# A fused cross-attention and spline feed-forward kernel: mask work moved in front of weight sums in batch 0, banks of value and stage products exchanged, late turning in the first quad, and the seventh product ahead of the next batch's first projections

## The reference, cut to what matters

```python
kv_c = kv @ W_kvc                                  # [512, 256] per batch
q_c = q @ W_dq                                     # [512, 384]; q is the normalised x
q_nope = (q_c @ W_uq).reshape(b, lq, H, HD)        # 16 heads of 128
q_rope = _rope((q_c @ W_qr).reshape(b, lq, H, R))  # R = 64
k_nope, v = kv_c @ W_uk, kv_c @ W_uv
k_rope = _rope(kv_c @ W_kr)
scores = (q_nope @ k_nope^T + q_rope @ k_rope^T) * scale
good = (k_ids <= qs) & (k_ids >= qs - LOOKBACK)    # qs: the token's segment number
attn = softmax(where(good, scores, NEG))
out = (attn @ v).reshape(b, lq, H * HD) @ W_o      # [512, 2048] @ [2048, 1024]
```

## Time and profile before

| | |
|---|---|
| runs | 3152.68, 3148.94, 3150.11 us; median 3150.11 |
| profiled execution | 3152.13 us, span of the core 3150.3 us |
| mean granted TensorE clock | 0.968 |
| busy share | PE 94%, DVE 69%, ACT 52%, POOL 30% |
| chain that ended last | 67% of it on PE, 9% DVE, 4% ACT, 1% POOL, 1% DMA |

### The profile page before, as it was taken

One profiled execution on the slowest core, in us unless ns is written; L12 is line 12 of the kernel. 1 busy time (PEld: TensorE's weight loads), 2 busy tenths in 40 slices (PEclk: granted clock), 3 DMA queues, 4 the chain that ended last, 5 costly groups with the idle time before them and its releaser, 6 DMA issues.

```text
span 3150.3 us, 41227 instructions
## 1 busy us (share of the span) xinstructions
PE 2960.7 (94%) x13886; PEld 2390.0 (76%) x13886; DVE 2181.1 (69%) x4546; ACT 1645.4 (52%) x3220; POOL 942.7 (30%) x685
## 2 busy tenths in 40 slices
PE   8899987999999999999999999999999999999985
PEld 6777766788778877788787887788777887878762
DVE  4555655777677775777667776677757777577776
ACT  3665634555365553655445553555526554465553
POOL 6355453221412114212332114112142212321127
PEclk9999998999999999999999999999999999999995
DMA  7565655555565546455664556655465555645432
GB/s 254 184 206 184 210 204 197 186 181 175 219 230 186 174 158 257 170 182 184 219 231 171 179 176 234 210 184 179 161 250 186 184 184 210 223 163 184 148 100 13
DMA packets 178303, 592.73 MB, mean 188 GB/s; under 512 B 38304, under 2 KB 52256, under 8 KB 141744
## 3 DMA queue, kind: packets, MB, share of 16 engines
q1 hardware_dynamic: 173024, 589.21, 53.8%
q0 software_dynamic: 5072, 0.88, 0.7%
HBM read 471.31 MB, written 85.14 MB: 177 GB/s over the span
## 4 chain that ended last, share of the span: by engine, by line
PE 67%; DVE 9%; ACT 4%; issue 2%; POOL 1%; DMA 1%; ACTq 0%; SPq 0%; POOLq 0%; DVEq 0%
PE psD L2577 8%; PE psA L2498 7%; PE psC L2594 7%; PE psB L2507 5%; PE psE L2594 5%; PE psT L2564 4%; PE psA L2450 3%; PE psS L2536 3%; PE psS L2537 3%; PE psS L2549 3%; PE psS L2545 3%; PE psS L2546 3%; PE psD L2520 2%; DVE probsT_lo L1897 2%; PE psB L2450 2%
## 5 line engine op out<-in xcount | busy, mean ns | idle before, releaser
L1459 ACT ACTIVATE exps_ring<-exps_ring,neg_max 128x512 f32<-128x512 f32 x512 | 370.9, 724 | 398.7 <-DVE neg_max L1885 397.6
L1885 DVE CUSTOM_DVE_ANT_0 exps_ring<-psS,mask 128x512 f32<-128x512 f32 x512 | 352.6, 689 | 173.3 <-PE psS L2549 155.1
L1473 ACT ACTIVATE probsT_hi<-psT 128x512 fp32r<-128x512 f32 x432 | 258.1, 597 | 410.6 <-PE psT L2564 406.8
L1897 DVE TENSOR_TENSOR probsT_lo<-psT,probsT_hi 128x512 fp32r<-128x512 f32 x432 | 297.5, 689 | 174.9 <-ACT probsT_hi L1473 173.4
L1465 ACT ACTIVATE exps_ring<-exps_ring,row_sum_inverse 128x512 f32<-128x512 f32 x512 | 368.6, 720 | 48.0 <-DVE row_sum_inverse L1891 47.9
L2594 PE MATMUL psC<-w_o_product,attn_product 128*128 128x512 f32 x1260 | 344.7, 409 | 24.5 <-POOL w_o_product L1095 23.8
L2594 PEld LDWEIGHTS psC<-w_o_product,attn_product 128*128 128x128 f32 x1260 | 228.3, 192 | 72.7 <-POOL w_o_product L1095 25.3
L2594 PE MATMUL psE<-w_o_product,attn_product 128*128 128x512 f32 x1008 | 272.4, 405 | 0.0
L2564 PE MATMUL psT<-ident,exps_ring 128*128 128x128 f32 x1728 | 261.7, 274 | 10.6 <-DVE probsT_lo L1897 9.7
L2564 PEld LDWEIGHTS psT<-ident,exps_ring 128*128 128x128 f32 x1728 | 210.1, 140 | 79.7 <-issue 33.6
L2498 PE MATMUL psA<-q_c_hi,w_uq_ring 128*128 128x512 f32 x768 | 262.7, 396 | 0.1
(11 more groups left out here) (488 smaller groups left out, 6612.1 us busy)
## 6 DMA issues: line engine op xcount, KB each, us to landing
w_o_product<-w_o_split SPq DMA_DIRECT2D x190, 1024.0 KB, 5.4
w_uq_ring<-w_uq_split SPq DMA_DIRECT2D x112, 384.0 KB, 4.7
w_o_split<-w_o_product SPq DMA_DIRECT2D x28, 1024.0 KB, 5.5
w_uk_ring<-w_uk_split SPq DMA_DIRECT2D x112, 256.0 KB, 2.9
w_uv_quad<-w_uv_split SPq DMA_DIRECT2D x28, 1024.0 KB, 6.9
w_qr_sorted<-w_qr_split SPq DMA_DIRECT2D x28, 768.0 KB, 4.3
x_stage<-in_x_dram SPq DMA_DIRECT2D x32, 512.0 KB, 5.2
x_stage<-in_ctx_dram SPq DMA_DIRECT2D x32, 512.0 KB, 6.0
```

The lines of the kernel that those rows point to most:

```text
L1459: act.activation(E[:, qt, :], E[:, qt, :], ACT.Exp, scale=-1.0, bias=mx[:, i % 2, qt:qt + 1], accum_out=rs[:, i % 2, qt:qt + 1]).then_inc( ...
L1885: dve.tensor_tensor_reduce(E[:, qt, :], psS[qt % 2][:, :], mask[:, qt, :], -SCALE, BIG, ALU.add, ALU.min, mx[:, i % 2, qt:qt + 1]).then_in ...
L1897: dve.tensor_tensor(PT[1][:, :, qt * P:(qt + 1) * P], turn_bank(q, i, qt)[:, :].rearrange("p (c n) -> p c n", c=TT), hi.bitcast(F32), ALU. ...
```

## The change

1. *Other banks.* Tile 1 of the values of quads 1 to 3 goes to psC in place of psE. In the stretch between batches, stage 0 is turned into psB and psA, stage 1 into psB and psE, stage 2 into psS0 and psS1; product (3,0,0) goes to psC and (3,0,1) to psA.
2. *Late turning.* In quad 0 the heads 1 to 3 (before: 1 and 2) make the next head's q and k ahead of turning their own probabilities. `product_hi(0, 0)` moves to the end of head (0, 3) on ACT.
3. *Between batches.* Stage 0 is turned inside head (3, 3), stage 1 right behind it, stage 2 before the last turned tile; product (2,6,1) moves into head (3, 3), ahead of (2,6,0). DVE makes norm_stats and norm_x of tile 2 inside head (3, 3). SP issues the load of tile 2 ahead of a weight load, that of tile 4 ahead of the w_dq loads.
4. *Product 6 of quad 3* moves in front of `into_heads`.
5. *Batch 0.* `wo_hi` of products 1, 3 and 5 moves behind q_hi and k_hi in its head; `wo_hi(q, 0)` moves to the end of head 3. Some loads, sums and norms of batch 1 come earlier. On POOL, `masks(1)` moves in front of `wo_lo(3, 4)` and `wo_sum(3, 4)`.

The core of the diff:

```diff
         def values_bank(q, kt):
             if q == 0:
                 return (psC, fullC, freeC) if kt % 2 else (psD, fullD, freeD)
-            return (psE, fullE, freeE) if kt == 1 else (psD, fullD, freeD)
+            return (psC, fullC, freeC) if kt == 1 else (psD, fullD, freeD)
...
+        def stage_bank(b, k):
+            return (psB, psA, psB, psE)[k] if b > 0 and k < 4 else stages[k % 4]
...
SP, end of head (3, 3) and between batches
+                        load_xs(b + 1, 2)
                         load_o(b, NQ - 1, 0)
-                        load_xs(b + 1, 2)
...
+                    load_xs(b + 1, 3)
                     if not first:
                         weights(1)
-                    load_xs(b + 1, 3)
+                    load_xs(b + 1, 4)
                     load_dq(b + 1)
...
POOL, body
                     if first:
-                        for j in range(3, 5):
-                            wo_lo(NQ - 1, j)
-                            wo_sum(NQ - 1, j)
+                        wo_lo(NQ - 1, 3)
+                        wo_sum(NQ - 1, 3)
                     masks(b + 1)
                     if first:
+                        wo_lo(NQ - 1, 4)
+                        wo_sum(NQ - 1, 4)
                         wo_lo(NQ - 1, 5)
...
ACT, head
-                    late = q0 and 1 <= i <= 2
+                    late = q == 0 and i > 0
                     if late:
-                        q_hi(b, q, i + 1)
-                        k_hi(b, q, i + 1)
+                        q_hi(b, *following)
+                        k_hi(b, *following)
...
-                    if i == HQ - 1 and not plain_quad(b, q):
+                    if i == HQ - 1 and q > 0 and not plain_quad(b, q):
                         product_hi(b, q, 0)
-                    if first and q > 0 and i < 2:
-                        wo_hi(q - 1, (1, 3)[i])
-                    if first and i == HQ - 1:
-                        wo_hi(q, 0)
...
+                    if i == HQ - 1 and q == 0:
+                        product_hi(b, q, 0)
...
DVE, head
+                    if at_end:
+                        stage_lo(b + 1, 0, False, 1)
...
+                    if at_end:
+                        norm_stats(b + 1, 2)
...
+                    if at_end:
+                        norm_x(b + 1, 2)
...
PE, values
                     wait_free(free, pos_v(b, q, kt))
-                    if q > 0 and kt == 1:
-                        pe.wait_ge(s_ptlo, tile_no(b, q, 0, 1) + 1)
...
PE, body
+                turn_stage(b + 1, 1, False)
                 turn_probs(b, o, HQ - 1, 2)
-                turn_stage(b + 1, 0, False)
-                product(b, o - 1, 6, 1)
+                turn_stage(b + 1, 2, False)
                 turn_probs(b, o, HQ - 1, 3)
                 product(b, o, 0, 0)
                 attend(b, o, HQ - 1)
-                turn_stage(b + 1, 1, False)
                 product(b, o, 0, 1)
-                turn_stage(b + 1, 2, False)
                 product(b, o, 1, 0)
                 product(b, o, 1, 1)
                 turn_stage(b + 1, 3, False)
...
                 product(b, o, 5, 0)
                 product(b, o, 5, 1)
-                into_heads(b + 1)
                 product(b, o, 6, 0)
                 product(b, o, 6, 1)
+                into_heads(b + 1)
```

More of the change, by code:

```diff
@@ L1639, in head @@
                     normalise(b, q, i, 2)
-                    if i < HQ - 1 and not late:
-                        q_hi(b, q, i + 1)
-                        k_hi(b, q, i + 1)
-                    elif nxt is not None:
-                        q_hi(b, nxt, 0)
-                        k_hi(b, nxt, 0)
+                    if following is not None and not late:
+                        q_hi(b, *following)
+                        k_hi(b, *following)
+                    if first and q > 0 and i < HQ - 1:
+                        wo_hi(q - 1, (1, 3, 5)[i])
                     if late:
@@ L2093, in head @@
                     head0 = q0 and i == 0
+                    following = (q, i + 1) if i < HQ - 1 else None if nxt is None else (nxt, 0)
+                    at_end = i == HQ - 1 and q == NQ - 1 and not last
                     vf = first and head0
```

178 lines of the change are left out of this document (100 added, 78 removed).

## The result

| | median us | runs | ratio to before, 95% interval |
|---|---|---|---|
| before | 3151.39 | 3148.94 to 3154.27, 4 runs | |
| after | 3101.86 | 3099.49 to 3104.81, 4 runs | 0.9843, 0.9826 to 0.9860 |

What follows compares the result with a forecast made beforehand. PE was taken as the bound, busy 2960.7 of 3150.3 us. The terms 20.2 + 4 + 16 + 13 - 5 = 48 off 3152.1 gave 3104.1, or 3102 against the median; range 3080 to 3128.

Steps and rivals of the forecast that it cites:

- Step 1: Values of tile 1 into psC: their wait for probsT_lo goes, gaining 20.2 us in batches 1 to 7, 6.3 in batch 0.
- the 0.96 itself: Idle time shown before tile 1 of the values, 21 times in batches 1 to 7, all counted as gain.
- Rival (d): The value bank changes nothing because another part is as late as probsT_lo was: 3122 us, chance 0.1.
- Step 2: Head (0, 3): q_lo wait of 1.91 us mostly shifts to product (0,0,0); net 0.6 a batch, 4 in seven.
- Rival (a): Late turning gains its whole wait, 1.91 us in all batches and 5.66 in batch 0: 3089 us, chance 0.13.
- Step 3: Inside batch 0: moved wo_hi shortens waits, with bank and clock gains: 6.3 + 2.2 + 2.9 + 4.6 = 16 us.
- wo_hi leaves the front of q_hi ... three times 0.95: Batch 0, quads 1 to 3: the scores' 2.23 us wait shrinks as wo_hi moves, gaining 2.9 us.
- the 4.6 of clock: Heads of batch 0: two or three half-clock stretches of 3.41 us should go, gaining 4.6 us.
- Step 4: Between batches: down_q, then held by its weights, gains 1.3 us and the clock 1.7, in each of six stretches.
- Step 5: Product 6 before into_heads: first scores newly wait 1.1 us for q_lo; net loss 0.8 each, 4.8 in six.
- The 0.28: Hold in us of the first scores' start at 1244.97 before the change, put down to the stack of rope queries.
- Step 6: Batch 0 to 1: masks delay wo_lo(4), the store and ctx loads; PE idles some 26 us, a loss of 5.

Runs made afterwards that it cites:

- x1: Kernel before with only tile 1 of the values of quads 1 to 3 moved to psC, no longer waiting for probsT_lo: 3114.17 us, ratio 0.9881.
- x2: Kernel after with late turning of head (0, 3) taken back and product_hi(0, 0) again in front of normalise 2 on ACT: 3112.35 us, ratio 0.9871.
- x8c: Kernel after, late turning kept, with product_hi(0, 0) before normalise 2 on ACT and product_lo(0, 0) before the turned low parts on DVE: 3086.67 us.
- x10c: Kernel after with all wo_hi of batch 0 back in their old places on ACT: 3083.26 us, ratio 0.9771.
- x6c: Kernel after with the w_dq_hi load cut into two halves, down_q taking the first halves before waiting for the second: 3095.53 us, ratio 0.9814.
- x11_all: Kernel after with old wo_hi places, early operand of product (0,0,0), product 6 behind into_heads, w_dq_hi in halves, POOL's short items between mask tiles: 3039.50 us.

## Why the prediction was right, and where its steps were not

**Step 1, values:** right in mechanism. The size was off in batches 1 to 7, 26 for 20.2; in batch 0 the idle time that went was 6.6 for 6.3. The failed term is the 0.96 itself: idle time in the rows leaves out the overlap of matmuls (0.17 us) and the slower start behind a wait (0.08). Rival (d) is ruled out by x1.

**Step 2, late turning:** right. The new wait was there at 1.52 (1.9 forecast), on the operand named; net 0.6 us a batch by x2. The clock, three dips in seven batches, made it 8.5 rather than 4 by x2 (6.6 by difference in the changed kernel's own heads, 32.6 less 26). Rival (a) is out as a result of this kernel, and x8c shows what it was worth.

**Step 3, batch 0:** wrong, by 13.5 us by this pair of traces and by 8 at the least given the scatter, in the term "wo_hi leaves the front of q_hi ... three times 0.95" and in the 4.6 of clock. It counted the wait that shrinks and not who waits for wo_hi: the turned tile behind it on ACT and the low parts on POOL, and with them the products. The stack of rope queries comes later as well, by a way that no run shows. x10c put a price on it, 17.3 us the other way in one pair of traces, some 13 between the groups, and 8.5 of idle time.

**Step 4, between batches:** right in what holds down_q, wrong in one wait, sizes small. The wait of 1.35 us for the low part of stage 0 in psB did not come: PE turns stage 1 into psB at 1156.08 without idle time, and so in all six stretches. The wait for norm_x(2) is 0.81 where 1.45 was forecast; attend came 2.4 us later, not 3.0. The weights are issued 1.1 us later (1.8 forecast) and land in 6.2 to 6.8 us where 7.0 was taken. So down_q starts 2.2 to 2.7 us earlier instead of 1.3, and waits 1.3 to 1.6 us for the weights' DMA (1.9 forecast). In the sixth stretch they took 8.9, and it lost 0.7. None of the five undisturbed stretches has PE below full clock any more, where one third of the loss was expected to stay. No run takes this part back alone, so that the new order and banks caused it is read from the traces. The rule of the Trainium skill on the shared ports ("SBUF — State Buffer", "Who interferes with whom") did not decide: norm_x(2), the one on the path, took 0.81 us beside an idle POOL; norm_x(3) took 1.81 at 1165.50 while POOL's sum of 1.28 ran from 1165.47, so it was 1.00 longer beside the 1.25 that the sum still ran. The rule would hold it for the whole rest; the trace shows most of it. Nothing waited for this norm_x.

**Step 5, product 6:** right, 0.96 of new wait (1.1 forecast), 0.7 to 1.2 net. The 0.28 that it puts down to the stack of rope queries stands under "issue" in its row; what held the scores there is not shown.

**Step 6, batch 0 to 1:** right chain, wrong start; the terms are the 6.2 us for the mask's input (2.7) and the start of POOL (2.4 us sooner). The forecast loss of 5 was a gain of 3.0.

**Sum:** 48 came out as 49.5 because the miss of step 3 (13.5 too much) met steps 1 and 2 (8.4 too little), steps 4 and 5 (3.2 too little) and step 6 (8 too little). The sum's closeness is luck: the steps missed by 33 us in all, and the misses cancel to 6. That the kernel is faster, and by the values, the late turning and the stretches between batches above all, is no luck.

**Left open:** why the load of w_dq_hi lands 6.3 us behind its issue in most batches and 7.6 to 8.9 in none to three of six, which ones changing from kernel to kernel. It can move a time by some 5 us, with the lower clock that follows a wait of 3 to 4 us. Also open: why the mask's input lands in 2.7 us in the one place where the masks were moved forward, why rope_hi is later in batch 0, and why PE is at half clock for 3.4 us or for 20.5 in heads of the same order. No run here was made to tell.

## What to carry to other kernels

When an instruction is moved behind another on its engine, list who waits for the moved one on every engine and queue before counting the wait that shrinks: here 2.9 us of forecast gain came with a loss of 13 to 17. Long work on one engine (four mask tiles, 29 us) is best cut, with the short items that others wait for between the pieces; putting it wholly in front or wholly behind came out within 2 to 4 us of each other, and in between gave 12 in the stretch. And do not pass over the small waits of the bounding engine where they repeat: the two that were measured cost 0.2 to 0.3 us more than their rows show. One trace against one trace prices a stretch only after the scatter of that stretch is known; where several runs leave it untouched, they give it.

## What the runs showed of the hardware

At the places that were taken out, PE idle time in a row understated what it cost: 0.96 shown was 1.2 to 1.3 lost, 1.52 shown was 1.6 to 1.8. Waits of about 2 us were followed by half the granted clock (1.2 GHz) in some batches and not in others of the same kernel (1.91 us: two of seven before, one of seven in x1, three of seven in x2). In front of down_q in batches 2 to 7 no wait from 1.3 to 1.7 us was, in any of the kernels with the new order, and of the 17 waits of 2.7 to 4.1 us there (x6c and x11_all, with the load in halves, left out) 13 were. A 2 KB DMA of POOL landed 6.1 us behind its issue with 234 GB/s moving around it (before, 450 to 458) and 2.6 us with 161 GB/s (after, 431.5 to 436); in the other batches of these two kernels it took 6.1 to 8.6. Traffic was not varied alone, so that it is the cause is not shown.
